# Two graph-attention layers, one core: the adjacency matrix is narrowed to bytes by a cast DMA and turned by transposing DMAs

## What is computed

```python
# layer 0: 4 heads of 32 columns
Wh = (h @ W).reshape(N, H, D)
e = leaky_relu(s_src[:, None, :] + s_dst[None, :, :], 0.2)
e = where(adj[:, :, None] > 0, e, NEG_INF)
x = layernorm(x + elu(einsum('ijh,jhd->ihd', softmax(e, axis=1), Wh)))
# layer 1: one head of 128 columns, on x_tan = logmap0(x)
scores = where(adj > 0, leaky_relu(wh1 + wh2.T, 0.2), NEG_INF)
x = layernorm(x + proj(expmap0(softmax(scores, axis=1) @ x_tan)))
```

## Time and profile before

| what | value |
|---|---|
| median of 2 runs | 1094.07 us (1094.0 to 1094.14) |
| span of the profiled execution | 1093.5 us |
| the runs' median less the span | 0.6 us |
| TensorE busy | 894.4 us, 82% |
| VectorE busy | 904.3 us, 83% |
| ScalarE busy | 609.9 us, 56% |
| GpSimd busy | 56.1 us, 5% |
| DMA moved | 85.88 MB, mean 79 GB/s |

### The profile page before, as it was taken

How to read it: one execution, slowest core, us unless ns; L and a number is a source line. 1 busy time by engine, 2 the same in 40 slices (tenths; PEclk the granted TensorE clock), 3 DMA queues, 4 the chain that set the end, 5 groups by cost and what they waited for, 6 DMA issues and landing times. The chain is left out here.

```text
span 1093.5 us, 27630 instructions
## 1 busy us (share of the span) xinstructions
PE 894.4 (82%) x11508; PEld 738.1 (68%) x11508; DVE 904.3 (83%) x1648; ACT 609.9 (56%) x672; POOL 56.1 (5%) x59
## 2 busy tenths in 40 slices
PE   2851799988899988999788970369899999999990
PEld 2751799988899888999778970335555555555550
DVE  0598798889998899988999986899888778778825
ACT  1736799996799957999556741344225135134101
POOL 1041000000000000000000000520000000000000
PEclk8885799999999989999999995679999999999996
DMA  8480736440664506640040003300321312303000
GB/s 194 90 224 0 232 65 132 99 99 22 203 128 98 99 2 213 136 99 22 1 175 21 2 2 78 99 1 1 97 58 40 90 32 73 87 10 96 0 10 11
DMA packets 47566, 85.88 MB, mean 79 GB/s; under 512 B 1298, under 2 KB 38612, under 8 KB 42708
## 3 DMA queue, kind: packets, MB, share of 16 engines
q0 software_dynamic: 4608, 33.56, 16.6%
q1 hardware_dynamic: 38612, 48.47, 13.9%
q10 hardware_dynamic: 4224, 2.10, 0.7%
HBM read 96.54 MB, written 21.14 MB: 108 GB/s over the span
## 5 line engine op out<-in xcount | busy, mean ns | idle before, releaser
L816 PE MATMUL bank<-moving,ring 128*128 128x99 bf16 (+1 forms) x6656 | 452.1, 218 | 22.9 <-DVE ring L777 21.8
L816 PEld LDWEIGHTS bank<-moving,ring 128*128 128x128 fp8e4 x6656 | 388.6, 98 | 25.3 <-DVE ring L777 12.8
L732 ACT ACTIVATE ring<-s_rows,scores 128x1024 fp8e4<-128x1024 f32 x320 | 340.5, 1140 | 108.7 <-PE bank L816 98.4
L1274 PE MATMUL bank<-moving,pair 128*128 128x387 bf16 x1792 | 300.1, 329 | 3.2 <-DVE evac L1363 3.2
L1274 PEld LDWEIGHTS bank<-moving,pair 128*128 128x128 fp8e4 x1792 | 175.8, 98 | 127.6 <-DVE evac L1363 3.6
L816 PE MATMUL bank<-moving,masks 128*128 128x99 bf16 x1536 | 209.8, 210 | 37.0 <-DVE evac L786 18.5
L816 PEld LDWEIGHTS bank<-moving,masks 128*128 128x128 fp8e4 x1536 | 151.7, 99 | 39.8 <-issue 31.1
L747 DVE TENSOR_SCALAR ring<-s_rows,neg_d 128x1024 uint8<-128x1024 f32 x192 | 131.4, 747 | 10.4 <-PE bank L816 6.9
L420 ACT ACTIVATE raw_masks<-bank 128x1024 fp8e4<-128x1024 bf16 x128 | 122.9, 1021 | 18.0 <-PE bank L412 16.5
L1201 ACT ACTIVATE small<-small 128x4 f32<-128x4 f32 x24 | 4.9, 205 | 219.3 <-DVE small L1147 180.6
L768 DVE SCALAR_TENSOR_TENSOR ring<-ring,masks 128x1024 int32<-128x1024 int32 x80 | 97.4, 1218 | 19.8 <-ACT ring L732 19.8
(11 more groups left out here) (218 smaller groups left out, 610.3 us busy)
## 6 DMA issues: line engine op xcount, KB each, us to landing
adj_tiles<-in_adj_dram POOLq DMA_DIRECT2D x32, 1024.0 KB, 8.5
masks_kept<-masks SPq DMA_DIRECT2D x4, 4096.0 KB, 13.0
pair<-masks_kept SPq DMA_DIRECT2D x8, 2048.0 KB, 9.8
s_rows<-score_rows SPq DMA_DIRECT2D x16, 512.0 KB, 3.7
values_kept<-masks SPq DMA_DIRECT2D x1, 2048.0 KB, 14.8
s_rows<-score_rows SPq DMA_DIRECT2D x8, 256.0 KB, 9.7
out_dram<-result ACTq DMA_DIRECT2D x8, 256.0 KB, 2.3
score_rows<-ring SPq DMA_DIRECT2D x1, 128.0 KB, 12.8
```

The source lines that it names most:

```text
L732: last = act.activation(below[:, k * C:(k + 1) * C], s_rows[:, h % 2, :], ACT.Sign, bias=scores[:, j, h:h + 1], saturate=False)
L816: last = pe.matmul(bank[b][:, at + lo:at + hi], mask, moving[:, j, h, lo:hi], start=first, stop=(j == T - 1), skip_group_check=True)
L1274: last = pe.matmul(bank[2 * t + side][:, 0:PARTS * K1], pair[:, y, side, j * R + t * P:j * R + (t + 1) * P], moving1[:, j, side * PARTS * ...
```

## The change

Nodes are dealt to partitions in pairs: node 256t + 2p + k is at partition p, in tile 2t + k. `x_rows`, `out_rows` and `adj_rows` follow this order, so that rows of x and of the output come in pieces of 1 KB where they were 512 bytes.

`shrink_adj` (GpSimd) copies the rows of a tile from DRAM to DRAM and casts int32 to fp8: 2 MB read, 0.5 MB written into `adj_small`; three of them may be in flight. Eight are issued in the preparation; the other 24 are issued from the start of the second block, with no wait on the chunks. `turn_adj` (SyncE) reads 256 rows of `adj_small` as 2048 columns of 2 bytes and has the DMA transpose them into `raw_masks`; a chunk has TURNS = 4, of 1 MB each. Each waits for its two narrowed tiles. For chunk 0 they stand in SyncE's queue behind the two loads of `s_rows`; for chunk c + 1, behind `keep(c)` and ahead of `load_s(c, 2)`.

A transposed element is a pair of bytes, for the column tiles 2t and 2t + 1. So the bytes of one tile now lie at a step of two in `masks`, `raw_masks`, `ring` and `pair`. ScalarE and VectorE write their bytes at that step and TensorE reads its stationary operand at it (`of_tile`, `of_run`); VectorE's word operations keep their shape. `clean_masks` shifts and masks in place of masking and setting the sign. The loads of masks in layer 1 come in pieces of 1 KB where they were 512 bytes.

TensorE's `turn_group` and ScalarE's `take_group` are gone, with `adj_tiles` and the four banks.

```diff
-    x_rows = x.rearrange("(t p) f -> p t f", p=P)
+    TT = T // 2
+    x_rows = x.rearrange("(t p k) f -> p t k f", p=P, k=2)
+    adj_rows = adj.rearrange("(t p k) j -> t k p j", p=P, k=2)
...
-        def load_adj(pool, b, t):
-            pool.dma_start(adj_tiles[:, t % 2, :], adj[bass.ds(b * C + t * P, P), :]).then_inc(adj_in[t % 2], 16)
-        def turn_group(pe, b, q):
-        ...
-        def take_group(act, b, q):
-        ...
+        def shrink_adj(pool, c, t):
+
+            n = c * CT + t
+            if t >= 3:
+                pool.wait_ge(small_adj_in[t - 3], 16 * c + 16)
+            elif c > 0:
+                pool.wait_ge(small_adj_in[CT + t - 3], 16 * c)
+            pool.dma_start(adj_small[n * P:(n + 1) * P, :], adj_rows[n // 2, n % 2, :, :]).then_inc(small_adj_in[t], 16)
+
+        def turn_adj(sp, c, k):
+
+            per = CT // TURNS
+            for t in range(per * k, per * (k + 1)):
+                sp.wait_ge(small_adj_in[t], 16 * c + 16)
+            size = C // TURNS
+            dst = raw_masks[:, :].bitcast(BF16).rearrange("p (t i) -> p t i", t=TT)
+            sp.dma_start_transpose(dst[:, :, k * size:(k + 1) * size],
+                                   adj_small[c * C + k * size:c * C + (k + 1) * size, :].bitcast(BF16))\
+                .then_inc(raw_in[k], 16)
...
             if g == 0:
-                dve.wait_ge(turned_out, b * Q + Q)
+                for k in range(TURNS):
+                    hold(dve, raw_in[k], b * 16 + 16)
...
-            dve.tensor_scalar(masks[:, :].bitcast(I32)[:, here], raw_masks[:, :].bitcast(I32)[:, here], TWOS, SIGNS,
-                              ALU.bitwise_and, ALU.bitwise_or).then_inc(mask_ready, 1)
+            dve.tensor_scalar(masks[:, :].bitcast(I32)[:, here], raw_masks[:, :].bitcast(I32)[:, here], 3, TWOS_NEGATIVE,
+                              ALU.logical_shift_left, ALU.bitwise_and).then_inc(mask_ready, 1)
...
+                for k in range(TURNS):
+                    turn_adj(sp, 0, k)
                 sp.wait_ge(values_out, 16)
...
-                load_adj(pool, 0, 0)
-                load_adj(pool, 0, 1)
...
-                for t in range(2, CT):
-                    pool.wait_ge(turned, (t - 1) * QT)
-                    load_adj(pool, 0, t)
+                for t in range(CT):
+                    shrink_adj(pool, 0, t)
...
-                last = act.activation(below[:, k * C:(k + 1) * C], s_rows[:, h % 2, :], ACT.Sign,
+                last = act.activation(of_tile(below, k, 0, C), s_rows[:, h % 2, :], ACT.Sign,
...
-                last = dve.tensor_scalar(below[:, k * C:(k + 1) * C], s_rows[:, h % 2, :], neg_d[:, h, j:j + 1],
+                last = dve.tensor_scalar(of_tile(below, k, 0, C), s_rows[:, h % 2, :], neg_d[:, h, j:j + 1],
...
-                    with pool.Fori(0, NC - 1) as c:
+                    for c in range(1, NC):
                         for t in range(CT):
-                            pool.wait_ge(turned, c * Q + (Q + (t - 1) * QT))
-                            load_adj(pool, c + 1, t)
+                            shrink_adj(pool, c, t)
...
-                    with sp.Fori(0, NC - 1) as c:
+                    for c in range(NC - 1):
                         keep(c)
+                        for k in range(TURNS):
+                            turn_adj(sp, c + 1, k)
                         load_s(c, 2, c * H + 1)
```

More of the change, by code:

```diff
@@ L29 @@
 TWO = 0x40
[L30 to L31 removed]
+TWOS_NEGATIVE = 0xC0C0C0C0 - (1 << 32)
 WIDEST = 150.0
@@ L56, in two_layer_gat @@
     T = N // P
-    x_rows = x.rearrange("(t p) f -> p t f", p=P)
-    out_rows = out.rearrange("(t p) f -> p t f", p=P)
+    TT = T // 2
+    x_rows = x.rearrange("(t p k) f -> p t k f", p=P, k=2)
+    out_rows = out.rearrange("(t p k) f -> p t k f", p=P, k=2)
+    adj_rows = adj.rearrange("(t p k) j -> t k p j", p=P, k=2)
     CT = 8
@@ L82, in two_layer_gat @@
     PIECES_AT = [3, 4, 5, 6, 11, 13]
-    EARLY = QT
-    ACT_GROUPS = 3
     ON_POOL = 1
[L86 to L94, removed]
+    TURNS = 4
     RT = 4
@@ L102, in two_layer_gat @@
     values_kept = nc.dram_tensor("values_kept", (P, T, F), F32, kind="Internal").ap()
-    masks_kept = nc.dram_tensor("masks_kept", (NC, P, T, C // 4), I32, kind="Internal").ap()
+    adj_small = nc.dram_tensor("adj_small", (N, N), FP8, kind="Internal").ap()
+    masks_kept = nc.dram_tensor("masks_kept", (NC, P, TT, C // 2), I32, kind="Internal").ap()
     ctx = ExitStack()
@@ L253, in _ @@
                                 sp.dma_start(v[:, :, :], values_kept).then_inc(loaded, 16)
-                            with sp.Fori(0, T) as it:
-                                sp.wait_ge(adj_used, it + 1)
-                                sp.dma_start(adj_tile[:, :], adj[bass.ds(it * P, P), :]).then_inc(adj_in, 16)
+                            with sp.Fori(0, TT) as it:
+                                for k in range(2):
+                                    sp.wait_ge(adj_used, it * 2 + (k + 1))
+                                    sp.dma_start(adj_tile[:, :], adj_rows[bass.ds(it, 1), k, :, :]
+                                                 .rearrange("o p j -> (o p) j")).then_inc(adj_in, 16)
                     @block.vector
@@ L384, in two_layer_gat @@
             "mean_ready", "exp_asked", "exp_given", "scores_out", "values_out")
-        adj_in = sems("adj_in0", "adj_in1")
-        a1_taken, turned, turned_out, mask_ready, kept, pool_done = sems(
-            "a1_taken", "turned", "turned_out", "mask_ready", "kept", "pool_done")
+        small_adj_in = sems(*(f"small_adj_in{t}" for t in range(CT)))
+        raw_in = sems(*(f"raw_in{k}" for k in range(TURNS)))
+        a1_taken, mask_ready, kept, pool_done = sems("a1_taken", "mask_ready", "kept", "pool_done")
         s_in = sems("s_head_in0", "s_head_in1")
@@ L393, in two_layer_gat @@
         pair_seen, cast_asked, cast_given, side_done = sems("pair_seen", "cast_asked", "cast_given", "side_done")
-        turn_bank = [bank[4 + i] for i in range(4)]
-        def load_adj(pool, b, t):
-            pool.dma_start(adj_tiles[:, t % 2, :], adj[bass.ds(b * C + t * P, P), :]).then_inc(adj_in[t % 2], 16)
-        def turn_group(pe, b, q):
[L402 to L413, removed]
@@ L472, in round_sides @@
         def round_sides(act):
-            left = list(range(EARLY + T // 2, Q))
             for pair in side_pairs:
@@ L807, in pe_chunk @@
                         j = g * JU + k
-                        mine = slice(k * C + t * P, k * C + (t + 1) * P)
+                        below_tile = of_tile(below, k, t * P, (t + 1) * P)
                         if DIRECT[u]:
-                            of_all = masks[:, j * C + t * P:j * C + (t + 1) * P]
-                            weighed = ((of_all, 0, PARTS * K0), (below[:, mine], 0, W0))
-                        else:
-                            weighed = ((above[:, mine], 0, PARTS * K0), (below[:, mine], PARTS * K0, W0))
+                            of_all = of_tile(masks[:, :], j, t * P, (t + 1) * P)
+                            weighed = ((of_all, 0, PARTS * K0), (below_tile, 0, W0))
+                        else:
+                            weighed = ((of_tile(above, k, t * P, (t + 1) * P), 0, PARTS * K0),
+                                       (below_tile, PARTS * K0, W0))
                         for mask, lo, hi in weighed:
@@ L877, in _, with part @@
                 with only_if(act, flag[0:1, 0:1], False):
-                    def part(c, units, build):
+                    def part(c, units):
                         for u in units:
                             act_unit(act, c, u)
[L881 to L887, removed]
+                    part(0, range(ROT))
                     with act.Fori(0, NC - 1) as c:
-                        part(c, range(ROT, U), True)
-                        part(c + 1, range(5), False)
+                        part(c, range(ROT, U))
+                        part(c + 1, range(5))
                         elu_exp(act, c)
-                        part(c + 1, range(5, ROT), False)
-                    part(NC - 1, range(ROT, U), False)
+                        part(c + 1, range(5, ROT))
+                    part(NC - 1, range(ROT, U))
                     elu_exp(act, NC - 1)
@@ L1202, in close_act @@
             act.wait_ge(result_ready, e + 1)
-            act.dma_start(out_rows[:, run_rows(e), :], result[:, y, :, :]).then_inc(stored[y], 16)
+            pairs = slice(e * RT // 2, (e + 1) * RT // 2) if isinstance(e, int) else bass.ds(e * (RT // 2), RT // 2)
+            act.dma_start(out_rows[:, pairs, :, :], result[:, y, :, :].rearrange("p (t k) f -> p t k f", k=2))\
+                .then_inc(stored[y], 16)
         with nc.Block() as block:
@@ L1240, in signs @@
                                 j = g * GT + k
-                                last = act.activation(pair[:, y, 1, j * R:(j + 1) * R], s_rows1[:, y, :], ACT.Sign,
```

(5 more changed lines are left out.)

64 lines of the change are left out of this document (17 added, 47 removed).

## The result

The changed kernel takes 1188.35 us (median of 2 runs, 1188.16 to 1188.54) against 1094.07: a ratio of 1.087, 95% interval 1.083 to 1.091. It is 8.7% slower, 28 us beyond the top of the range.

What follows compares the result with a forecast made beforehand. No engine alone was taken to bound layer 0; without mask work a chunk is bound by VectorE. 1094 + 1 (preparation) - 27.5 (chunks) + 28 (stall) + 0 (step) = 1095.5, with late rows 1097 us; range 1068 to 1160.

Steps and rivals of the forecast that it cites:

- The new wait in SyncE's queue, chunk 0: Head 2's row of scores, behind four transposing DMAs, lands at 201 us; TensorE stalls 31 us, taken as 28.
- T: Time of one transposing DMA of 1 MB, shown by no profile row: taken as 5 us, range 3 to 10.
- the one-for-one rule: Profile reading while x loads, between 7 and 14 us: casting queue sent 175 packets and SyncE's 171, one for one.
- the preparation: Before chunk 0: tile wait of 4.43 us and eviction wait of 0.98 us go, x lands 7 us later; net +1 us.
- the chunks' gain: Layer 0 without transposes and evictions: chunk 0 gains 11 us, chunks 1 and 2 gain 8.6 and 7.8; sum -27.5 us.
- late rows in chunks 1 and 2: Head 2's row behind `keep` and transposing DMAs: 0 us counted at 5 us per DMA; a small share lifts 1095.5 to 1097.
- Rival 2: Slow transposing DMAs keep SyncE's ring full before `load_s`: chunk 0 stalls about 54 us, chunks 1 and 2 13 each; 1151 us; chance 0.28.
- rival 3: In the preparation, x lands behind the narrowing copies in 2 KB packets, 23 us later: 16 us more, 1113 us; chance 0.08.
- the main case: Mask work leaves the chunks, returns as a stall at chunk 0's head 2; x 7 us later; 1083 to 1115 us; chance 0.46.
- the step of two: Bytes of TensorE, ScalarE and VectorE at that step: taken as 0, up to +90 us; as a rival 1169 us, chance 0.06.
- Layer 1: From 651 us on, no turning and only byte steps change; its loads and the output gain at most a few tenths.
- Rival 4: No stall: a narrowing copy priced by the 0.5 MB written, 2.8 us, so head 2's row is in time; 1067 us; chance 0.12.

Runs made afterwards that it cites:

- Experiments 1 and 4: Changed kernel, single runs. 1: a chunk's narrowing copies wait for the previous chunk's transposing DMAs, 1111.4 us; 4: each copy cut into four DMAs of 1024 columns, 1167.7 us.
- experiment 9: Kernel before, without the adjacency loads, transposes and evictions within the chunks, every chunk using chunk 0's masks: 1075.5 us, ratio 0.984.
- experiment 5: Changed kernel with first copy waiting for x, later copies waiting for the previous chunk's transposing DMAs, and four score-row buffers: 1060.05 us, ratio 0.970.

## Why the prediction was wrong

**The step that failed** is in "The new wait in SyncE's queue, chunk 0": "Then the fourth DMA and the row of scores run one for one with the copies for chunk 2, about 2T and 6 (3.7 when alone)". I had read the one-for-one rule off and used it for x; for the transposing DMAs I counted contention as a doubling of their time, and the first three's at T each. By the rule, with packets of 256 bytes, 1 MB is 4096 packets, 256 for each of 16 engines, and each waits for one of 624 ns: some 160 us for a DMA that takes 5 alone. The first DMA landed after 112.5, at 262.9, since the copies had run out by 262, and SyncE was free of it after 107, with 2909 of its 4096 packets sent. The row that I had landing at 201 came at 278, and the stop was 93 us where I had 28. Of the 91 us between 1097 and 1188 the stop is 65, the preparation 15 and the chunks' gain 12; the 1.5 us kept for late rows in chunks 1 and 2 weren't needed. I had even written that T might be more "if pieces get shorter", but asked only what short pieces cost alone, not beside long ones. Experiments 1 and 4 show both halves: without copies beside them 5 us, and with the neighbour's packets cut to a quarter 32 to 43 in place of 107. In a smaller slip, the count as written gives a stop of 51.5 us for T = 9 and 56.5 for T = 10, where the text has 54 and 60.

**T itself was right.** The transposing DMAs hold SyncE for 4.9 us each when alone and land in 8.2; I took 5. The Trainium skill, "DMA: Bandwidth & Descriptors", "Latency and other measured facts", gives 261 GB/s, by which an estimate is 4.0 us. The measured 4.9 are 214 GB/s, and the trace decides; about a quarter of these 4.9 us are gaps between one DMA and the next, and outside them the queue moved some 290 GB/s (chunk 1, 389 to 404 us). By an estimate of 2.8 us the sum would have been 1086, not the recorded 1082. Rival 2 named the right place and the wrong cause: chunks 1 and 2, where it put 26 us, show no stop at head 2. No copies run in them. Behind `keep`'s 4 MB the first transposing DMA of chunk 1 held SyncE for 15.1 us, the others for 4.3 to 5.0.

**x** came out as rival 3 had it: 23.4 us later at TensorE (forecast of the rival 23, of the main case 7), though by another count, so that the match in the number is luck: x went in 2048 packets of 1 KB, not 1024 of 2 KB. SyncE's queue had sent 932 packets by 8 us, beside 62 of the copies', and the rest went at 27 a us beside the copies. Chunk 0 started 16.1 us later. 7.3 us of the delay were made up in between, where I had 5.4 (the 4.43 of the tile load and the 0.98 of the eviction; the cleaning waits for nothing now).

**The chunks' gain** was too high. I set chunks 1 and 2 to the last chunk's 129.4; they came to 134.6 and 132.5, and 133.8 and 131.9 in experiment 9. The last chunk isn't followed by another: by its end no work has been done for a next one. VectorE was busy 122.4 us in its window and 128.4 in chunk 1's, with four comparisons, two word operations and three cleanings fewer. Chunk 0 was estimated at 119 and takes 122. Together the chunks gained 16 us instead of 27.5.

**Right as forecast:** the step of two costs nothing, as rule and rows had it. The Trainium skill, "Vector Engine (DVE) Microarchitecture Reference", section 5.1, whose condition for the two-port mode asks for no step of one, agrees with 751 ns against 747. Layer 1 is unchanged. The stop stands where I put it, at unit 16 of chunk 0.

**Rival 4** priced a copy by the bytes that it writes, 2.8 us. Alone on the engines a copy takes 4.9 (526 packets in 18 us of experiment 5, 144 to a copy), 430 GB/s read. It writes half of what the cast load writes in nearly the same time (5.67), so its price goes with the bytes read.

## What to carry to other kernels

In these runs a queue's progress beside another was counted in packets: take the number of its packets on an engine times the duration of the other queue's packet, not its bytes. A DMA of small pieces must be kept apart in time from copies of long rows, by a wait of its own, and nothing urgent may stand behind it in the same issuing queue. A chunk that lacks the work to be removed is a good gauge for the rest only if it also does the others' work for the chunk that follows; the last one doesn't.

## What the runs showed of the hardware

- Two DMA queues shared the 16 engines packet for packet, to within one in a few thousand: 2543 to 2543 with packets of 4096 and 256 bytes written, 7887 to 7888 with 1024 and 256.
- A transposing DMA of 1 MB occupies the sequencer that issues it for nearly its whole length: 4.9 us with nothing beside it (the median of 16), 107 us beside the copies, while an ordinary store of 4 MB was issued in 0.36 us.
- x's rows in pieces of 512 bytes had gone in packets of 2 KB (171 packets, 0.35 MB), in pieces of 1 KB they went in packets of 1 KB: the longer pieces made twice as many packets.
